# Scores of a sliding-window attention as 64x64 array tiles of 192 keys, with the keys kept as an older and a newer block

## What is computed

```python
w = n // WINDOW                                  # blocks of 128 queries
bq = q.reshape(b, h, w, WINDOW, d) * QK_SCALE
bk = k.reshape(b, h, w, WINDOW, d)
bk, bv = look_around(bk), look_around(bv)        # previous block and own block: 256 keys
sim = einsum('bhwid,bhwjd->bhwij', bq, bk)
mask = (i < j) | (i > j + WINDOW) | (j == -1)    # i, j: positions of query and key
sim = where(mask, -max, sim)
out = einsum('bhwij,bhwjd->bhwid', softmax(sim), bv)
```

## Time and profile before

| | us |
|---|---|
| median of 3 runs | 3447.11 (3445.01 to 3450.86) |
| the profiled execution | 3447.14 |
| its span, first to last instruction | 3445.3 |
| TensorE matmul busy | 3331.9 (97%) |
| TensorE weight load busy (beside matmul) | 2585.0 (75%) |
| VectorE busy | 2360.8 (69%) |
| ScalarE busy | 2128.0 (62%) |
| GpSimd busy | 2109.8 (61%) |
| granted TensorE clock, mean | 0.991 |

### The profile page before, as it was taken

The page is one execution under the profiler, slowest core; times in us unless marked ns, Lnnn a source line. Parts: engine busy times, 40 slices in busy tenths (PEclk is TensorE's granted clock), DMA queues, the critical chain, the costliest instruction groups (busy, mean ns, idle before and its releaser), DMA issues.

```text
span 3445.3 us, 80516 instructions
## 1 busy us (share of the span) xinstructions
PE 3331.9 (97%) x24412; PEld 2585.0 (75%) x24412; DVE 2360.8 (69%) x7850; ACT 2128.0 (62%) x5246; POOL 2109.8 (61%) x2124
## 2 busy tenths in 40 slices
PE   5999999799999999999999999999999999999998
PEld 3666666477777787878777777787777787778777
DVE  5999999556666666666666666666666666666664
ACT  3556555366666666666666666666666666666665
POOL 3888888555555555555555556666666666666664
PEclk8999999899999999999999999999999999999999
DMA  7111111000000000000000001111111111111110
GB/s 225 57 44 44 46 44 43 27 21 23 23 23 23 21 24 22 23 23 23 23 23 23 23 23 35 35 35 36 35 36 35 36 35 36 35 36 35 36 35 29
DMA packets 152912, 124.76 MB, mean 36 GB/s; under 512 B 22564, under 2 KB 148888, under 8 KB 152224
## 3 DMA queue, kind: packets, MB, share of 16 engines
q1 hardware_dynamic: 146352, 110.67, 10.5%
q10 hardware_dynamic: 6128, 8.86, 0.8%
HBM read 77.44 MB, written 42.02 MB: 35 GB/s over the span
## 4 chain that ended last, share of the span: by engine, by line
PE 80%; DVE 9%; issue 7%; POOL 2%; DMA 1%; DVEq 0%; ACT 0%; SPq 0%; POOLq 0%; ACTq 0%
PE bank L534 26%; PE bank L708 18%; PE bank L541 12%; PE bank L716 10%; PE bank L688 7%; PE bank L668 7%; DVE shared L1023 2%; DVE a_den L1012 1%; DVE z L978 1%; DVE a_den L1010 1%; DVE a_moments L1043 1%; DVE a_moments L967 1%; DVE shared L1004 1%; DVE gated L1038 0%; POOL shared L1220 0%
## 5 line engine op out<-in xcount | busy, mean ns | idle before, releaser
L1269 POOL TENSOR_TENSOR shared<-shared,share_of 128x512 f32<-128x512 f32 x512 | 522.0, 1040 | 1011.0 <-DVE share_of L1121 1011.0
L534 PE MATMUL bank<-WQKV,xT 128*128 128x512 f32 x1536 | 706.0, 596 | 1.0 <-ACT xT L731 1.0
L708 PEld LDWEIGHTS bank<-zT,W 128*128 128x128 f32 x5632 | 648.9, 192 | 61.0 <-issue 59.8
L731 ACT ACTIVATE shared<-bank 128x512 f32<-128x512 f32 (+1 forms) x640 | 347.6, 553 | 519.7 <-PE bank L541 378.0
L708 PE MATMUL bank<-zT,W 128*128 128x128 f32 x5632 | 649.6, 275 | 0.9 <-ACT zT L891 0.9
L871 ACT ACTIVATE shared<-shared,negmax 128x256 f32<-128x256 f32 x1024 | 506.0, 496 | 1.6
L534 PEld LDWEIGHTS bank<-WQKV,xT 128*128 128x128 f32 x1536 | 283.4, 191 | 256.1 <-issue 247.7
L1256 POOL TENSOR_TENSOR rnorm<-clamped,HALF 128x8 f32<-128x8 f32 x256 | 420.3, 1642 | 76.2 <-DVE clamped L1094 64.3
L1112 DVE CUSTOM_DVE_ANT_0 shared<-bank,MASK 128x256 f32<-128x256 f32 x1024 | 375.6, 421 | 71.7 <-issue 71.7
L1109 DVE MEMSET spare<- 128x1 f32 x512 | 30.2, 59 | 417.8 <-PE bank L668 412.8
L541 PEld LDWEIGHTS bank<-IDENT,shared 128*128 128x128 f32 x2176 | 249.4, 141 | 82.8 <-DVE shared L1017 64.6
(11 more groups left out here) (132 smaller groups left out, 6145.9 us busy)
## 6 DMA issues: line engine op xcount, KB each, us to landing
X<-xl_rows SPq DMA_DIRECT2D x128, 128.0 KB, 2.2
X<-in_x SPq DMA_DIRECT2D x64, 128.0 KB, 2.2
x_tiles<-ax SPq DMA_DIRECT2D x64, 128.0 KB, 1.7
xl_rows<-axl SPq DMA_DIRECT2D x64, 128.0 KB, 1.7
XS<-xl_rows SPq DMA_DIRECT2D x128, 64.0 KB, 2.1
xm_rows<-X SPq DMA_DIRECT2D x128, 64.0 KB, 1.6
xs<-xm_rows SPq DMA_DIRECT2D x128, 64.0 KB, 1.8
xl_rows<-X SPq DMA_DIRECT2D x64, 128.0 KB, 1.7
```

Source lines behind the costliest of these rows:

```text
L534: mm = nc.tensor.matmul(held(tile, key)[:, 0:cols], lhsT[c], rhs[c], start=(c == 0), stop=(c == len(lhsT) - 1))
L708: mm = nc.tensor.matmul(held(tile, key)[:, k * P:(k + 1) * P], W1[:, tile.l, c, at:at + P], zT[:, c], start=(c == 0), stop=(c == KC - 1))
L731: return nc.scalar.activation(dst, src, ACT.Copy)
L1269: G.tensor_tensor(probs, probs, share_of[:, h:h + 3:2].unsqueeze(2).to_broadcast((P, 2, 2 * WINDOW)), ALU.mult).then_inc(done[f"share{b}"], 1)
```

## The change

- **Scores.** One step `score` of 16 matmuls for a tile. Each takes 64 rows (one head of a pair), 64 queries (one half of the block) and 192 keys: keys 0 to 191 for the first half of the queries and 64 to 255 for the second. The output of a half lies in its own 64 partitions of the bank. The quarter of each score square that no matmul writes holds what was there; the mask covers it. All PSUM banks are set to zero at the start, and TensorE waits for that ahead of its first matmul.
- **Keys.** The ring becomes an older and a newer block. A new step of ScalarE, `age_k`, copies the newer block (128x512) onto the older; keep_k then writes the newer one. The values stay in their ring, and weigh reads the older slot first. The mask is then the same for all tiles but the first of a stream; `MASK` has five parts.
- **Waits.** A new step `ready_score` claims all four score banks and waits for keep_q and keep_k. turn_z is cut in its two transposes, `turn_z_first` ahead of ready_score and `turn_z_last` between ready_score and the scores.
- **Order and banks.** `ORDER_L` and `BANK_L` are new. turn_p1, turn_p2 and turn_p3 move from the slot of the scores to the next (depth 2), norm, root_x and add_b2 from depth 2 to 3, add_f and finish from 3 to 4, keep_p1 and keep_p3 to depth 2.

```diff
-    "PE": [(1, "turn_q"), (3, "turn_z"), (2, "weigh3"), (2, "weigh0"), (2, "weigh1"), (2, "weigh2"), (1, "score0"),
-           (1, "score1"), (0, "turn_x"), (2, "project_o"), (0, "project_k"), (3, "widen0"), (3, "widen1"), (3, "widen2"),
-           (1, "turn_p3"), (0, "project_q"), (0, "project_v"), (0, "turn_k"), (3, "narrow"), (1, "turn_p0"), (1, "turn_p1"),
-           (1, "turn_p2")],
+    "PE": [(2, "turn_p2"), (1, "turn_q"), (2, "turn_p1"), (2, "turn_p3"), (3, "turn_z_first"), (1, "ready_score"),
+           (3, "turn_z_last"), (1, "score"), (2, "weigh2"), (2, "weigh0"), (2, "weigh1"), (2, "weigh3"), (0, "turn_x"),
+           (3, "widen2"), (0, "project_k"), (3, "widen0"), (3, "widen1"), (2, "project_o"), (0, "project_q"), (0, "project_v"),
+           (0, "turn_k"), (1, "turn_p0"), (3, "narrow")],
+    "ACT": [(0, "age_k"), (2, "keep_p2"), (1, "keep_q"), (3, "affine"), (1, "exp1"), (0, "keep_x"), (1, "exp3"), (1, "exp0"),
+           (2, "keep_o"), (0, "square_k"), (1, "exp2"), (3, "gelu"), (0, "square_q"), (0, "keep_v"), (0, "keep_k"),
            (1, "keep_p0")],
+    "DVE": [(4, "add_f"), (3, "norm"), (2, "keep_p1"), (2, "keep_p3"), (1, "max1"), (1, "max3"), (1, "max0"), (1, "max2"),
+           (1, "invert1"), (1, "invert3"), (1, "invert0"), (0, "sum_k"), (0, "rotate_k"), (1, "invert2"), (3, "gate0"),
+           (3, "gate1"), (2, "add_o"), (3, "gate2"), (0, "sum_q"), (0, "rotate_q"), (2, "stats")],
+    "POOL": [(3, "root_x"), (3, "add_b2"), (4, "finish"), (1, "share1"), (1, "share3"), (1, "share0"), (0, "root_k"),
+           (0, "add_k"), (0, "scale_k"), (1, "share2"), (0, "root_q"), (0, "scale_q")],
...
+            def ready_score(tile):
+                for p in range(PAIRS):
+                    claim(pe, tile, f"sim{p}")
                 after(pe, done["keep_q"], tile)
+                after(pe, done["keep_k"], tile, per=2)
+
+            def score(tile):
+                for g in range(2):
+                    for k in range(2):
+                        for half in range(2):
+                            for e in range(2):
+                                rows = slice(e * LD, (e + 1) * LD)
+                                queries = slice(half * LD, (half + 1) * LD)
+                                keys = kring[tile.seq][rows, 2 * g + k].rearrange("p o t -> p (o t)")[:, half * LD:half * LD + 3 * LD]
+                                at = k * 2 * WINDOW + half * LD
+                                mm = nc.tensor.matmul(held(tile, f"sim{2 * g + e}")[queries, at:at + 3 * LD], qT[rows, 2 * g + k, queries],
+                                                      keys, start=True, stop=True)
+                                if k == 1 and half == 1:
+                                    mm.then_inc(filled[f"sim{2 * g + e}"], 1)
...
+            def age_k(tile):
                 after(act, filled[last_score], tile, back=STREAMS)
...
+                copy(kring[tile.seq][:, :, 0], kring[tile.seq][:, :, 1]).then_inc(done["keep_k"], 1)
+
+            def keep_k(tile):
+                after(act, filled["kT"], tile)
+                after(act, done["keep_k"], tile, per=2, ahead=-1)
+                copy(kring[tile.seq][:, :, 1], held(tile, "kT")[:].rearrange("p (a t) -> p a t", a=PAIRS)).then_inc(done["keep_k"], 1)
...
+            for k in range(BANKS):
+                ins = V.memset(bank[k][:], 0.0)
+            ins.then_inc(consts_ready, 1)
...
-                now = MASK[:, 1:3] if tile.s < STREAMS else MASK[:, 0:2]
+                now = MASK[:, 2:4] if tile.s < STREAMS else MASK[:, 0:2]
```

More of the change, by code:

```diff
@@ L72 @@
-    "DVE": [(1, "max1"), (1, "max3"), (1, "max0"), (1, "max2"), (1, "invert1"), (2, "add_o"), (1, "invert3"), (0, "sum_k"),
-           (0, "rotate_k"), (1, "invert0"), (1, "invert2"), (2, "stats"), (1, "keep_p3"), (3, "gate0"), (3, "gate1"),
-           (3, "gate2"), (0, "sum_q"), (0, "rotate_q"), (2, "norm"), (3, "add_f"), (1, "keep_p1")],
-    "POOL": [(1, "share1"), (1, "share3"), (0, "root_k"), (0, "add_k"), (0, "scale_k"), (1, "share0"), (1, "share2"),
-           (2, "root_x"), (0, "root_q"), (0, "scale_q"), (2, "add_b2"), (3, "finish")],
+    "PE": [(2, "turn_p2"), (1, "turn_q"), (2, "turn_p1"), (2, "turn_p3"), (3, "turn_z_first"), (1, "ready_score"),
+           (3, "turn_z_last"), (1, "score"), (2, "weigh2"), (2, "weigh0"), (2, "weigh1"), (2, "weigh3"), (0, "turn_x"),
+           (3, "widen2"), (0, "project_k"), (3, "widen0"), (3, "widen1"), (2, "project_o"), (0, "project_q"), (0, "project_v"),
+           (0, "turn_k"), (1, "turn_p0"), (3, "narrow")],
@@ L638, in _, with turn_x_first, turn_x_last @@
             pe.wait_ge(layers_loaded, 16 * LAYER_LOADS)
+            def turn_x_first(tile):
+                after(pe, loaded[tile.seq], tile, back=tile.s % STREAMS + 1 - STREAMS, per=8)
+                turn(tile, "x", [X[tile.s][:, 0:P]])
+            def turn_x_last(tile):
+                nc.tensor.transpose(held(tile, "x")[:, P:2 * P], XS[tile.s % 4][:], IDENT[:]).then_inc(filled["x"], 1)
             def turn_x(tile):
-                after(pe, loaded[tile.seq], tile, back=tile.s % STREAMS + 1 - STREAMS, per=8)
-                turn(tile, "x", [X[tile.s][:, 0:P], XS[tile.s % 4][:]]).then_inc(filled["x"], 1)
+                turn_x_first(tile)
+                turn_x_last(tile)
             def project_qkv(key, tile):
@@ L694, in project_o, with turn_z_first, turn_z_last @@
                 project(tile, "wo", [oT[:, c] for c in range(PAIRS)], [WO[:, tile.l, c] for c in range(PAIRS)], D)
+            def turn_z_first(tile):
+                after(pe, done["norm"], tile)
+                turn(tile, "z", [z[:, 0:P]])
+            def turn_z_last(tile):
+                nc.tensor.transpose(held(tile, "z")[:, P:2 * P], z[:, P:2 * P], IDENT[:]).then_inc(filled["z"], 1)
             def turn_z(tile):
-                after(pe, done["norm"], tile)
-                turn(tile, "z", halves(z)).then_inc(filled["z"], 1)
+                turn_z_first(tile)
+                turn_z_last(tile)
             def widen(m, tile):
@@ L721, in _ @@
             steps.update({f"project_{k}": partial(project_qkv, k) for k in "qkv"})
-            steps.update({f"score{g}": partial(score, g) for g in range(2)})
+            steps.update({"ready_score": ready_score, "score": score, "turn_x_first": turn_x_first, "turn_x_last": turn_x_last,
+                          "turn_z_first": turn_z_first, "turn_z_last": turn_z_last})
             steps.update({f"turn_p{p}": partial(turn_p, p) for p in range(PAIRS)})
@@ L909, in gelu @@
                         ins.then_inc(done[f"gelu{m // 2}"], 1)
-            steps = {"keep_x": keep_x, "square_q": partial(square, 0), "square_k": partial(square, 1), "keep_v": keep_v, "keep_k": keep_k,
+            steps = {"keep_x": keep_x, "square_q": partial(square, 0), "square_k": partial(square, 1), "keep_v": keep_v, "keep_k": keep_k, "age_k": age_k,
                      "keep_q": keep_q, "keep_o": keep_o, "affine": affine, "gelu": gelu}
```

40 lines of the change are left out of this document (12 added, 28 removed), and 10 rows, old and new, of tables (BANK_L, FILLS).

## The result

| | before | after |
|---|---|---|
| median of 5 runs, same chip | 3446.21 us (3444.43 to 3450.86) | 3431.65 us (3429.58 to 3432.8) |
| ratio | | 0.9952, 95% interval 0.994 to 0.9963 |
| the profiled execution | 3447.14, span 3445.3 | 3429.58, span 3427.8 |

The account below looks back on a forecast made before the run. TensorE's chain was taken to bound the kernel: 126 slots x 0.43 = 54.2 us off, 1.6 back at the end and 0.5 at loop edges, so 52 off 3447, forecast 3395 us. The range was 3384 to 3436.

Follow-up runs that it names:

- e1: The changed kernel with 64 more long-met waits in TensorE's program ahead of stage L, shifting its loops in the instruction stream: 3412.2 us, ratio 0.9884.
- e2: The changed kernel with 128 more long-met waits in TensorE's program ahead of stage L: 3433.55 us (one run).
- e4: The changed kernel with the old score step, 8 matmuls of 64 rows, 128 queries and 256 keys, in the new order: 3475.03 us (one run).
- e5: The changed kernel with the first transpose of z done twice, ahead of ready_score: 3414.75 us (one run).
- e12: The new scores in the previous kernel's step order and bank plan, with the two query halves of a head next to each other: 3394.82 us (one run).
- e9: The new scores in the previous kernel's step order and bank plan, with stage L written without loops on TensorE alone: 3400.78 us, ratio 0.986.

## What to carry to other kernels

Where one engine bounds the kernel and its code runs in loops, an edit that adds or removes instructions on it can move the time by 19 to 25 us of 3430 by the loop's place alone: read every loop's edges before judging an edit, and compare versions with a pad or without loops. A margin between one engine's end and another's start must hold the hand-over, 0.25 us here from ScalarE to TensorE, and a wait of that size shows in the distance of starts, not as idle time. When one engine's edge is removed, look for the next engine's: taking away only TensorE's loops made this kernel slower.

## What the runs showed of the hardware that was not expected

- A loop edge of TensorE costs 1.4 to 2.7 us over a slot, or 4.5 to 7.1 us when the loop starts at certain places in its code (a second stand of 2.06 to 2.35 us in the rows above); seven edges of 3.6 to 3.9 lie between the two (in e1, e2, e4, e5 and e12) and show no second stand of TensorE, and their cause wasn't followed. How the place sets it is inferred; what holds the code back there isn't seen. ScalarE's edge is 2.72 us in e9's row.
- Row and column halves of the array work together in float32: 32 instructions of 64x64 by 192 columns in 1.46 us, by 256 columns in 1.89. The fixed part is 0.17 us in both (1.29 and 1.72 of streaming).
- Tiles run together only if their matmuls stand near each other: 1.46 us with them within four matmuls, 2.16 with the column halves eight apart; in that step a matmul starts ahead of three earlier ones (0.72 us in).
